# The last 2048 rows of a masked softmax-sum: the 0/1 mask as the stationary operand, high, low and weights as 258 moving columns

## The reference

```python
h = relu(layernorm(x))
H = h @ W_fc + b_fc
scores = (H @ w_att[:128])[:, None] + (H @ w_att[128:])[None, :] + b_att
scores = where(adj > 0, scores, -1e9)
out = x + softmax(scores, axis=1) @ H
```

## Time and profile before

| | |
|---|---|
| device time, median of 3 runs | 186.33 us (186.32 to 186.36) |
| the profiled execution | 186.24 us |
| its span, first to last instruction | 184.3 us |
| adjacency moved | 64 MB in 36 pairs, 2.0 or 1.5 MB each |
| TensorE busy | 160.3 us (87%) |
| VectorE busy | 124.9 us (68%) |
| ScalarE busy | 79.6 us (43%) |

### The profile page before, as it was taken

How to read it: one execution, slowest core, us unless ns; L and a number is a source line. 1 busy time by engine, 2 the same in 40 slices (tenths; PEclk the granted TensorE clock), 3 DMA queues, 4 the chain that set the end, 5 groups by cost and what they waited for, 6 DMA issues and landing times.

```text
span 184.3 us, 2691 instructions
## 1 busy us (share of the span) xinstructions
PE 160.3 (87%) x866; PEld 115.3 (63%) x866; DVE 124.9 (68%) x360; ACT 79.6 (43%) x232; POOL 10.7 (6%) x33
## 2 busy tenths in 40 slices
PE   0639859989499999989899999999999998999970
PEld 0326638666386867656668667686786775887750
DVE  0995696947999556788865569496594624459931
ACT  2567894999395052222251422442224424021020
POOL 2103601000130020000000000000000000000000
PEclk9999987999969999999999999999999999999995
DMA  5999999999999999999999999999999999998212
GB/s 144 410 439 432 412 443 420 434 420 430 427 430 432 412 441 411 441 420 428 420 422 424 427 427 424 422 427 423 425 424 427 437 431 427 411 398 329 76 60 59
DMA packets 8369, 71.63 MB, mean 389 GB/s; under 512 B 929, under 2 KB 1698, under 8 KB 3490
## 3 DMA queue, kind: packets, MB, share of 16 engines
q1 hardware_dynamic: 7776, 71.18, 92.3%
q10 hardware_dynamic: 578, 0.26, 0.5%
HBM read 69.34 MB, written 2.10 MB: 388 GB/s over the span
## 4 chain that ended last, share of the span: by engine, by line
DMA 59%; PE 23%; DVE 10%; issue 2%; ACT 2%; SPq 1%; DVEq 0%
DMA ring<-adj 59%; PE bank L844 9%; PE bank L850 8%; DVE mask L514 5%; PE bank L868 3%; PE bank L892 2%; PE bank L882 1%; DVE low L537 1%; ACT mask L456 1%; DVE mask L523 1%; ACT weighted L363 1%; SPq L271 1%; DVE x_sb L639 1%; DVE x_sb L646 1%; SPq L277 0%
## 5 line engine op out<-in xcount | busy, mean ns | idle before, releaser
L514 DVE TENSOR_SCALAR mask<-ring 128x1024 fp32r<-128x1024 int32 (+2 forms) x69 | 63.1, 934 | 41.6 <-DMA ring<-adj 37.1
L844 PE MATMUL bank<-mask,high 128*128 128x512 f32 x256 | 80.7, 418 | 11.0 <-DVE mask L514 6.3
L850 PE MATMUL bank<-mask,low 128*128 128x512 f32 x256 | 76.3, 401 | 0.0
L844 PEld LDWEIGHTS bank<-mask,high 128*128 128x128 f32 x256 | 47.8, 196 | 31.1 <-DVE mask L514 12.9
L850 PEld LDWEIGHTS bank<-mask,low 128*128 128x128 f32 x256 | 49.8, 194 | 11.1
L456 ACT ACTIVATE mask<-ring,half_steep 128x512 fp32r<-128x512 int32 x43 | 28.9, 718 | 62.1 <-DMA ring<-adj 60.6
L868 PE MATMUL bank<-mask,w_cols 128*32 128x512 bf16 x256 | 19.7, 392 | 2.3 <-ACT lines L422 2.3
L868 PEld LDWEIGHTS bank<-mask,w_cols 128*32 128x32 bf16 x256 | 5.9, 94 | 13.1 <-issue 8.7
L363 ACT ACTIVATE weighted<-relu,w_over_std 128x128 f32<-128x128 f32 x32 | 10.1, 391 | 4.7 <-DVE w_over_std L608 4.5
L374 ACT ACTIVATE relu<-x_sb,neg_mean 128x128 f32<-128x128 f32 x32 | 9.8, 388 | 3.2 <-DVE neg_mean L546 3.2
L389 ACT ACTIVATE high<-x_sb,neg_mean 128x128 fp32r<-128x128 f32 x24 | 9.3, 387 | 0.0
(11 more groups left out here) (85 smaller groups left out, 67.7 us busy)
## 6 DMA issues: line engine op xcount, KB each, us to landing
ring<-adj SPq DMA_DIRECT2D x18, 2048.0 KB, 17.1
ring<-adj SPq DMA_DIRECT2D x16, 1536.0 KB, 12.9
ring<-adj SPq DMA_DIRECT2D x3, 1024.0 KB, 9.3
out<-x_sb SPq DMA_DIRECT2D x7, 256.0 KB, 13.8
x_sb<-x SPq DMA_DIRECT2D x1, 1024.0 KB, 20.7
ring<-adj SPq DMA_DIRECT2D x4, 256.0 KB, 16.2
x_sb<-x SPq DMA_DIRECT2D x2, 256.0 KB, 3.8
x_sb<-x SPq DMA_DIRECT2D x1, 512.0 KB, 10.1
```

Of the source, the lines that this page charges most:

```text
L514: nc.vector.tensor_scalar(mask[:, n % MASKS, 0:cols], ring[:, n // 2 % RING, begin:begin + cols], 0.0, None, ALU.is_gt).then_inc(masks_rea ...
L844: nc.tensor.matmul(bank[:, b, :], high[:, t, :], mask[:, n % MASKS, cols], start=(t == 0), stop=False)
L850: last = nc.tensor.matmul(bank[:, b, :], low[:, t, :], mask[:, n % MASKS, cols], start=False, stop=(t == T - 1))
```

## The change

The first 16 row tiles (2048 rows) keep their layout. The other 2048 rows come in groups of 6, 6 and 4 tiles of 128 rows. For these, the 128 x 128 mask of (column tile, row tile) is the stationary operand, and one matmul moves 258 columns: `features[:, t, :, :]`, which holds the high features and the high part of the weight (129 columns), then the low ones (129). Rows of the output now stand on partitions, one row tile per PSUM bank, and no separate weight matmul is made for them. A unit of the groups of 6 is two tiles t (1536 mask columns), one of the last group four (2048 columns): 32, 16, 16 and 8 units, again 72 in 36 pairs of the same sizes in the same order.

To get from the sums of a row tile (rows on partitions) to the product with `w_sb`, ScalarE copies the 258 columns to `sums` (VectorE the very last), TensorE turns the high and the low part with `ident` as the moving operand, both into one PSUM region, which adds them (`turn`), ScalarE copies the result to `turned_sums`, and TensorE multiplies with `w_sb` (`row_products`). VectorE adds the two parts of the weight sums.

```diff
-GROUPS = [(0, 4), (4, 3), (7, 1)]
+GROUPS = [(0, 16), (16, 6), (22, 6), (28, 4)]
+BANKS = [None, [6, 0, 1, 2, 3, 4], [6, 0, 1, 2, 3, 4], [0, 1, 2, 3]]
+STEPS = [1, 2, 2, 4]
...
+    def share_of(n):       # columns of a unit's mask that ScalarE makes
+        return 0 if n not in SHARED else BLOCK if UNITS[n][0] == 0 else 2 * BLOCK
...
+    def closes(n):
+        return 0 < UNITS[n][0] < LAST_GROUP and local_of(n) >= COUNT[UNITS[n][0]] - 2
...
+            def row_sum_of(n, i, b):
+                g, t0, _ = UNITS[n]
+                t = t0 + i
+                if t == 0:
+                    bank_free(g, b)
+                at = (i * GROUPS[g][1] + b) * P
+                last = nc.tensor.matmul(bank[:, BANKS[g][b], 0:WIDE], mask[:, n % MASKS, at:at + P],
+                                        features[:, t, :, :].rearrange("p h d -> p (h d)"), start=(t == 0), stop=(t == T - 1))
...
+            def by_rows(n):        # two units, one row tile after the other
+                masks_of(n)
+                masks_of(n + 1)
+                for b in range(GROUPS[g][1]):
+                    for m in (n, n + 1):
+                        for i in range(step):
+                            last = row_sum_of(m, i, b)
...
+            def turn(k):
+                for m in range(2 if k % 2 else 4):
+                    nc.tensor.matmul(bank[:, OUT_BANK, m * P:(m + 1) * P], sums[:, first + m, 0:D], ident[:], start=True, stop=False)
+                    last = nc.tensor.matmul(bank[:, OUT_BANK, m * P:(m + 1) * P], sums[:, first + m, D + 1:WIDE - 1], ident[:],
+                                            start=False, stop=True)
...
+                elif local == 0 or closes(n):
+                    by_rows(n)
+                else:
+                    by_tiles(n)
+                    by_tiles(n + 1)
...
+                if g == 2:
+                    if local in (4, 8):
+                        turn((local - 4) // 4)
+                    if local in (6, 10):
+                        row_products((local - 6) // 4)
+                if g == 3:
+                    if local == 0:
+                        turn(2)
+                    if local == 2:
+                        row_products(2)
+                        turn(3)
+                    if local == 4:
+                        row_products(3)
+            by_tiles(LAST - 1)
+            for i in range(PER):
+                pe.wait_ge(last_masks_ready, i + 1)
+                for b in range(PER):
+                    row_sum_of(LAST, i, b)
...
+            for m in range(PER):   # waits for copies of sums left out here
+                nc.tensor.matmul(bank[:, DEN_BANK + m, 0:P], sums[:, m, 0:D], ident[:], start=True, stop=False)
+                nc.tensor.matmul(bank[:, DEN_BANK + m, 0:P], sums[:, m, D + 1:WIDE - 1], ident[:],
+                                 start=False, stop=True).then_inc(turned, 1)
+            for m in range(PER):
+                pe.wait_ge(turned_ready, 4 + m + 1)
+                nc.tensor.matmul(bank[:, m, 0:D], turned_sums[:, m * P:(m + 1) * P], w_sb[:],
+                                 start=True, stop=True).then_inc(row_products_done, 1)
```

More of the change, by code:

```diff
@@ L257, in unit_landed, with mask_free @@
                 engine.wait_ge(pair_landed[pair % RING], 16 * (pair // RING + (pair % RING > 0)))
+        def mask_free(engine, n):
+            before = n - MASKS
+            if before < 0:
+                return
+            if UNITS[before][0] == 0:
+                engine.wait_ge(fours_done, before // 4 + 1)
+            elif closes(before):
+                engine.wait_ge(row_sums_done, rows_before(UNITS[before][0] + 1))
+            else:
+                engine.wait_ge(units_done, sum(UNITS[m][0] > 0 and not closes(m) for m in range(before + 1)))
         block = ctx.enter_context(nc.Block())
@@ L459, in _, with share @@
-            act.wait_ge(half_steep_ready, 1)
[L460 to L472, removed]
+            def share(n):
+                begin, cols = n % 2 * COLS[n], COLS[n]
+                part = share_of(n)
+                unit_landed(act, n)
+                mask_free(act, n)
+                nc.scalar.activation(mask[:, n % MASKS, cols - part:cols], ring[:, n // 2 % RING, begin + cols - part:begin + cols],
+                                     ACT.Sigmoid, bias=half_steep[:], scale=STEEP).then_inc(shares_ready, 1)
@@ L630, in inverse_of @@
[L630 to L639 removed]
+                r0, width = GROUPS[g]
@@ L642, in result_of @@
                 dve.wait_ge(products_done, k + 1)
-                for m in range(PER):
-                    row = x_sb[:, k * PER + m, :]
-                    col = slice(m * width + b, m * width + b + 1)
-                    last = nc.vector.scalar_tensor_tensor(out=row, in0=bank[:, OUT_BANK + k % 2, m * D:(m + 1) * D],
-                                                          scalar=inv_den[:, col], in1=row, op0=ALU.mult, op1=ALU.add)
-                    if done is last_results_ready:
-                        last.then_inc(done, 1)
@@ L784, in _ @@
                 for t in range(T):
[L785 removed]
+                    last = nc.vector.scalar_tensor_tensor(out=features[:, t, 1, 0:D], in0=relu[:, t, :], scalar=1.0, in1=v_rows[:, 0, :],
                                                           op0=ALU.mult, op1=ALU.mult, accum_out=s_logit[:, t:t + 1])
@@ new lines, in row_products @@
+            def row_products(k):
+                pe.wait_ge(turned_ready, k + 1)
+                if k == 0:
+                    pe.wait_ge(mean_H_ready, 1)
+                else:
+                    pe.wait_ge(row_products_read, k)
+                for m in range(2 if k % 2 else 4):
+                    last = nc.tensor.matmul(bank[:, SMALL_BANK, m * D:(m + 1) * D], turned_sums[:, m * P:(m + 1) * P], w_sb[:],
+                                            start=True, stop=True)
+                last.then_inc(row_products_done, 1)
```

439 lines of the change are left out of this document (263 added, 176 removed).

## The result

| | before | changed |
|---|---|---|
| median, 9 runs each | 185.79 us (185.47 to 186.36) | 187.60 us (187.38 to 189.02) |
| ratio | | 1.0112, 95% interval 1.0086 to 1.0138 |
| profiled execution, span | 186.24, 184.3 us | 189.02, 187.2 us |

The forecast was 185.4 us, faster; the range ended at 187.3. The changed kernel's nine times form two sets: five from 187.38 to 187.60 and four from 188.79 to 189.02. The profiled execution belongs to the upper one.

What follows compares the result with a forecast made beforehand. Bound: DMA up to 154.50, TensorE for 22 us, then a serial end. From 186.24 us, minus 0.65 (last group) and 0.27 (end) gives 185.3; the median's 0.09 makes 185.4 us, range 184.7 to 187.3.

Steps and rivals of the forecast that it cites:

- The bound, and the part before 154.50: DMA sets the pace up to 154.50; pairs land as before, at 149.60 and 154.50, so earlier work costs nothing.
- The start of the last group: TensorE waits for both masks instead of one, starting at 156.93 instead of 155.78: a loss of 1.15 us.
- The pace p: Time per 258-column matmul in TensorE's stream: taken as 0.116 us, kept between 0.1115 and 0.1225.
- rival 3: Stationary loads do not hide: 0.226 us per matmul, TensorE bounds the second half, some 225 us; chance 0.03.
- The last sum: End of TensorE's last-group stream, start, matmuls and passes summed: 176.05 instead of 176.70, minus 0.65 us.
- Rival 2: No gain, about 186.2 to 186.5 us: slower matmuls or added waits use up the last group's saving; chance 0.17.
- The end: From the last sum's end, called E, to the end of the results: E + 3.6 instead of 3.89, minus 0.27.
- the late quarters: VectorE's last four quarter masks wait behind an earlier result; cover 0.5 us, anything beyond lost one for one.
- the masks: A late mask could starve the load queue and make the pairs land later; the forecast had masks in time.
- the queue: VectorE's added work has the ring between it and the load queue, three pairs, some 11 us: costed at nothing.
- Rival 1: TensorE's clock falls to 1.2 GHz in the last group after a wait: plus 1.65, 187.0 us; chance 0.33.
- The first of the two waits: TensorE, done near 150.3, waits 1.7 us for ScalarE's shares, to about 152.0, before closing the pair landed at 149.60.

Runs made afterwards that it cites:

- experiment 10: Kernel before, with the first sums of the last group waiting for the masks of both first units: 187.32 us, ratio 1.0096.
- experiment 3: Changed kernel, with the first two units of the last group done tile by tile, waiting for one mask: 186.31 us, ratio 1.0025.
- experiment 2: Changed kernel, with TensorE's branch at the end held until all result stores have landed: 185.74 us, ratio 1.0001.
- 6: Changed kernel, with TensorE's branch after the stores and the last group's first two units tile by tile: 184.31 us, ratio 0.9904.
- 7: Kernel before, with TensorE's branch held until all stores have landed: 185.63 us, ratio 0.9982.
- 1: Changed kernel, with eight unused float32 matmuls ahead of the last group's first sums: 187.43 us, ratio 1.0094.
- 9: Changed kernel, with eight unused matmuls ahead of the last group and TensorE's branch after the stores: 185.92 us, ratio 0.9987.
- experiment 5: Kernel before, with a wait for results and six unused matmuls ahead of TensorE's branch at the end: 186.45 us, ratio 1.0025.
- 8: Changed kernel, last group by tiles, TensorE's branch held to the last result, ScalarE's wait for stores behind its own branch: 182.87 us, ratio 0.9839.

## Why the prediction was wrong

**The bound, and the part before 154.50: right.** The pairs landed at 149.7 and 154.6, 0.1 later than before, and the work of the first three groups moved nothing.

**The start of the last group: right.** 157.07 against 156.93 foretold; experiment 10 prices the wait for both masks alone at 1.2 us (1.15 foretold), experiment 3 takes 1.2 back. It is the one term of the sum that is an outright loss of the change.

**The pace p: right in kind, too low.** 3.83 / 32 = 0.120 us, where I took 0.116 and allowed 0.1225. The loads hide (rival 3 is out), but the 15 ns are nearly a cost for each matmul, and halving the columns doubles it: 128 x 0.004 = 0.5 us. The estimate of 0.110 by the Trainium skill's formula (TensorE: Matmul & The Clock Gate, section Back-to-back issue gap) was further off. The last sum, without the clock's fall, ended at 178.21 - 1.49 = 176.72 instead of 176.05: the 0.65 that the last group was to gain came to nothing. With the branch moved and no fall it ends at 176.60 (experiment 2). Rival 2, no gain, had it right for this part: with a pace of 0.120 and waits a little longer than summed, the stream of the last group pays back its late start and no more.

**The end: right to 0.2.** From the last sum to the last result it took 3.76, foretold 3.6.

**The step that failed** is the one the prediction put as "then a serial end: ... and 3.7 us of stores to the end of the span at 184.3", and then carried over unchanged: "The end is E + 3.6, minus 0.27". It took the distance from the last result to the end of the program as a constant. The prediction took all of it for stores; the last one lands 2.2 us after the last result, and the other 1.5 are ScalarE's flag and branch. And the distance holds a coincidence of the kernel before: there TensorE is done 1.8 us ahead of the last result, because VectorE adds the means between, and its branch and the 16 KB packet behind it are nearly through before the stores. The change makes TensorE's last product wait for the last turned tile, ends it with the results, and puts the packet on the stores. Measured: 5.26 instead of 3.72 in the profile, 2.2 us between the lower sets with and without it (experiment 2) and 2.0 between experiments 3 and 6, 0.3 to 0.5 for the same edit in the kernel before (7).

Without this cost the time lies in the range: 185.74 in experiment 2, its lower set at 185.0 to 185.4 where the forecast was 185.4; with the upper set beside it that is no change against 186.0, not the gain foretold. That the lower set meets the forecast is luck: in its profile the last sum ends 0.55 us later than foretold, while the end without the packet is 0.5 shorter than the 3.7 carried over. The forecast also stood on three runs at 186.33; nine have their median at 185.79. Two terms were wrong, then: the stores by 1.54 us and the last sum by 0.67, most of it the pace. The prediction had nothing of the stores among its rivals; it had listed the late quarters, the masks and the queue as what could go wrong, and looked at no engine after its last matmul.

**Rival 1 was right, beside the forecast rather than in its place.** The fall came after the wait for the second mask, cost 1.49 us in the profile and 1.3 between the sets (1.65 foretold), and, by the upper set, happened in four of nine runs (0.33 foretold as a chance). The first of the two waits it named did not arise: TensorE was done with the pair before at 151.7, not 150.3, and waited 0.32 us there, not 1.7. (In the trace before, the two falls began 1.5 us after the end of the one wait and right at the end of the other, at 26.6 and 50.5; the prediction had read 1.7 and 0.2 after.) Taking the long wait away (3), filling it (1, 9) and making it alone (10) move the upper set as the theory says.

The traces show one more such wait, which the prediction did not name: 1.82 us, up to 124.2 to 124.5, where the changed kernel closes its second group and the masks stand behind results on VectorE. In experiment 2 the clock fell behind it, at 124.7. The loads set the pace there and the last group still began at 156.92, but TensorE came later to it, waited 0.97 us instead of 1.90, and no fall followed. In the changed kernel's profile the clock did not fall at 124 and fell at 158. The wait alone does not decide, for in experiment 10 one of 1.88 was followed by none; what does was not tried.

**What stays open.** In the changed kernel the packet falls behind the issues, and the last 16 data packets wait for its end. In the kernel before and in experiment 5 it falls on the issues and slows these. Why it slows them was not tried, and only these places were measured, not the way between.

## What to carry to other kernels

Read the trace past the last computing instruction of every engine, branches and instruction packets too: a branch over a long body at the end loads code by DMA, and if it falls beside the last stores it can cost more than the edit gains. Let the engine that finishes last wait for the last result before it branches, and put the wait for stores behind the branch; here the two gave 1.3 us to the old kernel and, with the start by tiles, 4.7 to the changed one. Do not make a bound TensorE wait for two masks where one will do: here it paid 1.2 us for the wait and, in part of the runs, 1.3 to 1.5 more for a lower clock behind it.

## What the runs showed of the hardware

A 16,384-byte instruction packet started 0.73 us after TensorE's branch in both kernels (0.7 to 1.3 in the others), took 1.3 to 1.7 us beside stores and 1.0 to 1.4 alone. Where it came behind the issues of the stores, 16 of their 512 packets started only at its end and the last landing was 3.6 to 3.7 us after the last issue instead of 1.6 (the changed kernel, experiments 1 and 3). Where it came among the issues, one took up to 1.22 us instead of 0.36. A wait of TensorE of 1.90 us was followed by 3.4 us of the 1.2 GHz level in the profile of the changed kernel, one of 1.88 in that of experiment 10 was not, nor were 0.97 and 0.71 in those of experiments 2 and 3. One of 1.82 us near 124 was followed by such a fall in experiments 2, 8 and 9 and not in the changed kernel, 1 and 3. Float32r matmuls with a 128 x 128 stationary operand each took 0.120, 0.177 and 0.2285 us for 258, 386 and 512 columns.
